# Turning all sixteen heads' probabilities by VectorE and memory in 23 of 48 attention items, with GpSimd making the context's low parts

## The chip, the cores and the metric

The kernel runs on one core of a Trainium2 chip. The metric is the device time of one execution, in microseconds, as the median of several runs. Beside it there is one profiled execution, in which every instruction of the five engines and the transfers are recorded; all rows below are from it.

## What is computed

Sixteen sequences of 128 tokens, width 512, go through a transformer block (self-attention, cross-attention, MLP) and then through a gated cross-attention. All three attentions have 16 heads of 32:

```
def attention(q, k, v, mask):
    scores = jnp.einsum('bhqd,bhkd->bhqk', q, k) / jnp.sqrt(jnp.float32(HD))
    scores = scores * mask - 10000.0 * (1.0 - mask)
    probs = jax.nn.softmax(scores, axis=-1)
    return jnp.einsum('bhqk,bhkd->bhqd', probs, v)
x = x + merge_heads(attention(q, k, v, ltor_mask)) @ w_ao + b_ao      # q, k, v from layernorm(x)
x = x + merge_heads(attention(q, k, v, cross_mask)) @ w_co + b_co     # k, v from the context
x = x + gelu(layernorm(x) @ w1 + b1) @ w2 + b2
out = x + tanh(gate) * (attention with layernorm(context) as k and v) @ Wo
```

## The kernel before

The work is cut into 48 attention items, one sequence in one layer each: items 0 to 15 are the first attention (phase A), 16 to 31 the second (B), then comes the MLP over all sequences, then 32 to 47 the third attention (D). The five engines each run a program written out by hand, and semaphores tie them together. Nothing is scheduled by a planner: the order on each engine is the order of the calls in its `step` function. A product in full precision is made of three: every operand is split into a high part (`context_hi` on ScalarE) and a low part (`context_lo`, which subtracts the high part from the whole), and high times high, high times low and low times high are summed.

A step g works on three items at once. TensorE multiplies the probabilities of item g-2 with v (`times_v`, line 835), makes the scores of item g (`scores`, line 776), projects q, k or v of a later pair of sequences (`project`, lines 750 and 758) with the row sums (line 810) and the transposes (`transpose_prob`, line 794) of item g-1 between, and ends with the output projection of item g-2 (line 858). VectorE masks the scores out of PSUM (line 1590), finds the row maxima (1603), inverts the row sums of item g-1 (`inverse_sums`, 1611), normalises the context of item g-2 (`context`, 1627) and makes its low part (`context_lo`, 1633). In phases A and B GpSimd adds the mask bias (2023) between the mask and the maximum. ScalarE takes 16 exponentials an item (1217), one a head, in four quarters.

Before probabilities can be multiplied with v, the 128x128 block of each head has to be transposed. There are two ways. For heads 0 to 7 ScalarE writes its exponentials into a tile `prob_blocks`, VectorE turns all 32x32 blocks in it with one instruction (`turn_blocks`, 1617), SyncE stores the tile to memory (`store_blocks`, 516) and reads it back with the blocks moved to their places (`bring_blocks`, four DMAs, 525). For heads 8 to 15 TensorE transposes in PSUM (8 instructions) and ScalarE copies the result back with one instruction (`probs_out`, 1194). Items in `BY_PE` use TensorE for all heads. The column order in which the first way leaves the probabilities is read by `times_v` with a stride (`by_head`).

SyncE issues all DMAs from one queue in program order; a wait in it holds everything behind. In step g its order around the change is: the result of item g-3 stored, the turned blocks of item g-1 read back, the row sums of item g-1 stored, the residual of item g-2 loaded, a layer-norm tile loaded in every second step, the row sums of item g-1 spread over the context tile (`spread_row_sums`, 559), then weights or masks, and last the blocks of item g stored and the next inputs read in transposed form.

```
def row_sums(g):
    pe.wait_ge(s_rt, g + 1)
    ...
def inverse_sums(g):
    par = g % 2
    dve.wait_ge(s_exp, 4 * g + 4)
def turn_blocks(g):
    dve.wait_ge(s_exp, 4 * g + 2)
```

## Time and profile before

| | |
|---|---|
| timed runs, median (lowest, highest) | 1100.44 us (1100.13, 1104.86) |
| profiled execution, span from first to last instruction | 1100.7 us |
| TensorE busy in the span | 1074.7 us, 98% |
| VectorE | 815.4 us, 74% |
| ScalarE | 712.7 us, 65% |
| GpSimd | 462.0 us, 42% |
| DMA, mean over the span | 152 GB/s |
| granted TensorE clock | full in every slice |

No time of its own is given for the profiled execution beside its span; the span is 0.3 us above the median of the timed runs. Busy shares are means over the whole span, in which the three attentions and the MLP follow one another; items 2 to 13 lie between 55 and 250 us, items 33 to 43 between 881 and 1055 us. The chain of waits is followed back from the last instruction, at each step to what released it. In the timeline a bracket gives the idle time ahead of a row and who ended it.

### The profile page before, as it was taken

What the parts mean: (1) busy time and instruction counts of PE and PEld (TensorE: products, weight loads), DVE (VectorE), ACT (ScalarE), POOL (GpSimd) and SP (SyncE); (2) the same over time, 40 slices, a digit from 0 to 9 for tenths busy, and PEclk for the clock granted to TensorE, in tenths of its full rate; (3) what the DMA queues carried; (4) which work ended last, traced back from release to release, by engine and by line L of the source; (5) the groups of instructions that cost most, each with busy time, mean ns of one, the idle gap of its engine ahead of it and who ended that gap; (6) DMA issues with size and microseconds to landing.
All of it is one profiled execution on the core that took longest, in us unless ns stands there. A gap on an engine that the chain in (4) does not pass through costs nothing.

```text
span 1100.7 us, 24328 instructions
## 1 busy us (share of the span) xinstructions
PE 1074.7 (98%) x8829; PEld 934.2 (85%) x8829; DVE 815.4 (74%) x1314; ACT 712.7 (65%) x2365; POOL 462.0 (42%) x337
## 2 busy tenths in 40 slices
PE   7989999999999999998999999999999999999998
PEld 6888888888888888886898888888888988888886
DVE  6678787778888778888877557656677478778777
ACT  4678777777788778786444434434444387777776
POOL 3665666557767776767512121103012331122100
PEclk9999999999999999999999999999999999999999
DMA  6366565576776777553241130220622146666633
GB/s 216 98 201 198 191 195 188 174 227 216 221 227 215 223 211 229 180 191 128 85 134 40 38 96 12 85 96 1 181 101 83 59 146 205 203 198 210 177 97 97
DMA packets 136135, 167.04 MB, mean 152 GB/s; under 512 B 16992, under 2 KB 82256, under 8 KB 136016
## 3 DMA queue, kind: packets, MB, share of 16 engines
q1 hardware_dynamic: 136016, 165.50, 47.9%
q8 instruction: 70, 1.15, 0.4%
q14 instruction: 49, 0.40, 0.1%
HBM read 113.15 MB, written 52.29 MB: 150 GB/s over the span
## 4 chain that ended last, share of the span: by engine, by line
PE 59%; DVE 12%; ACT 9%; POOL 7%; issue 4%; DMA 3%; SPq 1%; DVEq 0%; ACTq 0%; POOLq 0%
PE psum L938 15%; PE psum L919 14%; PE psum L758 13%; POOL prob L2023 6%; PE psum L858 5%; PE psum L750 5%; ACT prob L1217 4%; ACT prob_blocks L1217 2%; PE psum L794 2%; PE psum L776 2%; DVE prob L1590 2%; DVE ln_tile L1528 2%; PE psum L835 2%; DVE negmax L1603 2%; ACT inputs_transposed L1255 2%
## 5 line engine op out<-in xcount | busy, mean ns | idle before, releaser
L758 PE MATMUL psum<-inputs_hi,weights_hi 128*128 128x256 f32 x768 | 223.7, 291 | 5.4 <-POOL inputs_lo L2014 2.5
L758 PE MATMUL psum<-inputs_lo,weights_hi 128*128 128x256 f32 x768 | 217.1, 283 | 0.0
L758 PE MATMUL psum<-inputs_hi,weights_lo 128*128 128x256 f32 x768 | 217.0, 283 | 0.0
L2014 POOL TENSOR_TENSOR inputs_lo<-inputs_transposed,inputs_hi 128x512 fp32r<-128x512 f32 x84 | 113.0, 1367 | 228.9 <-DVE inputs_hi L1563 168.4
L2023 POOL TENSOR_TENSOR prob<-prob,mask_bias 128x1024 f32<-128x1024 f32 x64 | 152.7, 2408 | 98.3 <-DVE prob L1590 96.3
L1217 ACT ACTIVATE prob<-prob,negmax 128x128 f32<-128x128 f32 x472 | 182.2, 391 | 0.5 <-DVE negmax L1603 0.5
L758 PEld LDWEIGHTS psum<-inputs_hi,weights_hi 128*128 128x128 f32 x768 | 146.7, 191 | 10.3 <-issue 2.8
L1603 DVE TENSOR_REDUCE negmax<-prob 128x8 f32<-128x1024 f32 x96 | 115.9, 1210 | 50.0 <-POOL prob L2023 50.0
L758 PEld LDWEIGHTS psum<-inputs_lo,weights_hi 128*128 128x128 f32 x768 | 147.0, 191 | 0.2
L758 PEld LDWEIGHTS psum<-inputs_hi,weights_lo 128*128 128x128 f32 x768 | 146.9, 191 | 0.0
L858 PE MATMUL psum<-weights_hi,context_parts 128*128 128x512 f32 x376 | 125.8, 393 | 0.4 <-ACT kT L1168 0.3
L1217 ACT ACTIVATE prob_blocks<-prob,negmax 128x128 f32<-128x128 f32 x296 | 114.4, 389 | 16.9 <-DVE negmax L1603 16.9
L1303 ACT ACTIVATE qT<-psum,columns 128x512 f32<-128x512 f32 (+1 forms) x80 | 46.2, 598 | 106.2 <-PE psum L919 106.2
L1687 DVE SCALAR_TENSOR_TENSOR kT<-kT,qT 128x512 f32<-128x512 f32 x64 | 46.9, 733 | 80.3 <-ACT kT L1308 80.2
L2026 POOL TENSOR_TENSOR residual<-residual,bias_rows 128x512 f32<-128x512 f32 x42 | 57.7, 1378 | 83.3 <-DMA residual<-stream 63.3
L1217 ACT ACTIVATION_READ_ACCUMULATOR prob<-prob,negmax 128x1 f32 x472 | 90.3, 191 | 0.0
L938 PE MATMUL psum<-weights_hi,hidden_parts 128*128 128x512 f32 x264 | 87.7, 392 | 1.1 <-DVE hidden_parts L1682 1.0
L1255 ACT ACTIVATE inputs_transposed<-inputs_transposed,columns 128x256 f32<-128x256 f32 x120 | 62.3, 591 | 37.2 <-DVE inputs_transposed L1535 37.0
L1989 POOL TENSOR_TENSOR weights_lo<-weights_whole,weights_hi 128x512 fp32r<-128x512 f32 x56 | 75.8, 1367 | 21.3 <-ACT weights_hi L1154 21.3
L858 PEld LDWEIGHTS psum<-weights_hi,context_parts 128*128 128x128 f32 x376 | 70.6, 188 | 16.5 <-ACT qT L1303 0.6
L938 PE MATMUL psum<-weights_hi,context_parts 128*128 128x512 f32 x248 | 81.8, 390 | 0.9 <-DVE context_parts L1682 0.9
L1590 DVE SCALAR_TENSOR_TENSOR prob<-psum,mask 128x512 f32<-128x512 f32 x128 | 79.2, 680 | 0.0
(124 smaller groups left out, 2600.3 us busy)
## 6 DMA issues: line engine op xcount, KB each, us to landing
prob_turned<-prob_blocks SPq DMA_DIRECT2D x37, 512.0 KB, 3.0
prob<-prob_turned SPq DMA_DIRECT2D x148, 128.0 KB, 3.3
weights_whole<-weights_in SPq DMA_DIRECT2D x72, 256.0 KB, 3.4
normalised<-ln_tile SPq DMA_DIRECT2D x30, 512.0 KB, 2.8
inputs_transposed<-normalised SPq DMA_DIRECT2D x120, 128.0 KB, 2.9
context<-row_sums_spread SPq DMA_DIRECT2D x188, 64.0 KB, 2.1
stream<-residual SPq DMA_DIRECT2D x42, 256.0 KB, 2.7
residual<-stream SPq DMA_DIRECT2D x42, 256.0 KB, 3.7
```

The costliest lines, as they stand in the source:

```text
L758: mm = pe.matmul(ps[:, bank, GT * part:GT * part + GT], w[:, slot, c, o], a[:, buf, c, :], start=c == 0 and i == 0, stop=c == KC - 1 and i ...
L858: mm = pe.matmul(ps[:, U_BANK + 1, :], a[0][:, cs], w[:, slot, c, :], start=c == 0 and i == 0, stop=c == KC - 1 and i == 2)
L919: mm = pe.matmul(out, w[:, slot, c, o], a, start=c == 0 and i == 0, stop=c == KC - 1 and i == 2)
L938: mm = pe.matmul(ps[:, accumulator(group, t), :], a[gb][:, tok], w[:, slot, (j * chunks + e) % 4, :], start=j == 0 and e == 0 and i == 0, ...
L1217: ins = act.activation(dst, src, ACT.Exp, bias=negmax[:, par, s:s + 1], accum_out=total[:, par, s:s + 1])
L1255: ins = act.activation(dst, src, ACT.Identity, bias=cols[:, b0 + c:b0 + c + 1], scale=cols[:, g0 + c:g0 + c + 1])
L1590: ins = dve.scalar_tensor_tensor(heads(P[:, 512 * c:512 * c + 512]), ps[:, S_BANK:S_BANK + 4, T * c:T * c + T], SCALE, other.unsqueeze(1). ...
L1603: dve.tensor_reduce(negmax[:, par, 8 * h:8 * h + 8], heads(prob[:, par, 1024 * h:1024 * h + 1024]), AX.X, ALU.max, negate=True).then_inc(s ...
L1989: pool.tensor_tensor(wlo[:, slot, c, :], raw[:, slot, c, :], whi[:, slot, c, :].bitcast(f32), ALU.subtract).then_inc(s_wlo, 1)
L2014: pool.tensor_tensor(lo, y, hi.bitcast(f32), ALU.subtract).then_inc(s_rlo if fill.ln is None else s_flo, 1)
L2023: pool.tensor_tensor(half, half, mb.unsqueeze(1).to_broadcast([128, 8, T]), ALU.add).then_inc(s_biased, 1)
L2026: pool.tensor_tensor(tile, tile, brow[:, ROW_SLOT[name], :], ALU.add).then_inc(s_resb, 1)
```

## The change

In the 23 items of `WHOLE` (2 to 13 and 33 to 43) heads 8 to 15 take the first way too. ScalarE writes their exponentials into a second tile, `second_prob_blocks`; VectorE turns it (`turn_second_blocks`) when the item's last quarter of exponentials is done, in the step after; SyncE stores it (512 KB) and reads it back (4 x 128 KB). TensorE's 8 transposes and ScalarE's copy go. The row sums use another PSUM bank and wait for the context of the item before, and `times_v` waits for the second reads. The low part of the context is made by GpSimd, at the start of its step, for items 1 to 13 and 32 to 43 (`LO_BY_POOL`).

```diff
+WHOLE = tuple((*range(2, 14), *range(33, 44)))
+LO_BY_POOL = tuple((*range(1, 14), *range(32, 44)))
...
+        second_blocks = sb("second_prob_blocks", [128, NH // 2 * T])
...
         def row_sum_bank(g):
-            return U_BANK if sums_late(g) else U_BANK + 1
+            return T_BANK + 1 if g in WHOLE else U_BANK if sums_late(g) else U_BANK + 1
...
+            def store_second_blocks(g):
+                n = second_number(g)
+                sp.wait_ge(s_turned2, n)
+                if n > 2:
+                    sp.wait_ge(s_moved2, 64 * (n - 2))
+                sp.dma_start(turned_second[n % 2], second_blocks[:, :]).then_inc(s_pst2, 16)
+
+            def bring_second_blocks(g):
+                n = second_number(g)
+                sp.wait_ge(s_pst2, 16 * n)
+                blocks = turned_second[n % 2].rearrange("(i k) (j n) -> j k i n", i=4, j=4)
+                for j in range(4):
+                    dst = prob[32 * j:32 * j + 32, g % 2, NH // 2 * T:].rearrange("p (i n) -> p i n", i=4)
+                    sp.dma_start(dst, blocks[j]).then_inc(s_moved2, 16)
...
                 if st.prev and g - 1 not in BY_PE:
                     bring_blocks(g - 1)
+                if g - 1 in WHOLE:
+                    store_second_blocks(g - 1)
                 if st.prev:
                     store_row_sums(g - 1)
                 if st.ends:
                     load_stream(g - 2)
                 if st.later and st.later.ln is not None and not ahead_ln and g:
                     load_tiles(st.later)
+                if g - 1 in WHOLE:
+                    bring_second_blocks(g - 1)
                 if st.prev:
                     spread_row_sums(g - 1)
...
                 pe.wait_ge(s_rt, g + 1)
-                if sums_late(g):
+                if g in WHOLE:
+                    pe.wait_ge(s_cx, 2 * g)
+                elif sums_late(g):
...
             def times_v(g):
-                pe.wait_ge(s_pta, copied_by_act(g, 1))
+                if g in WHOLE:
+                    pe.wait_ge(s_rc, g + 1)
+                    pe.wait_ge(s_moved2, 64 * second_number(g))
+                else:
+                    pe.wait_ge(s_pta, copied_by_act(g, 1))
...
-                    else:
+                    elif g - 1 not in WHOLE:
                         transpose_prob(g - 1, 2)
                         if g != 44:
                             transpose_prob(g - 1, 3)
                 if not late:
-                    if st.prev:
+                    if g - 1 in WHOLE:
+                        u_bank_free(g)
+                    elif st.prev:
                         row_sums_out(g - 1)
...
+                second = g in WHOLE and quarter >= 2
+                if second and quarter == 2 and second_number(g) > 1:
+                    act.wait_ge(s_pst2, 16 * (second_number(g) - 1))
...
-                elif st.prev and g != 44:
+                elif st.prev and g != 44 and g - 1 not in WHOLE:
                     probs_out(g - 1)
...
+            def turn_second_blocks(g):
+                dve.wait_ge(s_exp, 4 * g + 4)
+                dve.transpose(second_blocks[:, :], second_blocks[:, :]).then_inc(s_turned2, 1)
...
                 if st.ends and not late:
                     inverse_sums(g - 1)
+                if g - 1 in WHOLE:
+                    turn_second_blocks(g - 1)
+                if st.ends and not late and g - 2 not in LO_BY_POOL:
                     context_lo(g - 2, 0)
                     context_lo(g - 2, 1)
...
             def step(st):
                 phase, b, g = st.phase, st.b, item(st)
+                if g - 2 in LO_BY_POOL:
+                    context_lo(g - 2, 0)
+                    context_lo(g - 2, 1)
                 if phase != D:
                     add_mask_bias(g, 0)
```

How the order moves, at three places. First VectorE in step 9 (context of item 7, row sums of item 8). Before:

```order
L1627 TENSOR_TENSOR context<-psum,context 128x256 x2
L1611 RECIPROCAL rtotal<-total 128x4x4
L1633 TENSOR_TENSOR context_parts<-context,context_parts 128x256 x2
L1590 SCALAR_TENSOR_TENSOR prob<-psum,mask 128x512 x4
L1603 TENSOR_REDUCE negmax<-prob 128x8
L1646 TENSOR_TENSOR v<-psum,bias_rows 128x512
L1603 TENSOR_REDUCE negmax<-prob 128x8
L1528 TENSOR_SCALAR ln_tile<-ln_tile,ln_mean_var,ln_rstd 128x512 x2
L1646 TENSOR_TENSOR v<-psum,bias_rows 128x512
L1617 STREAM_TRANSPOSE prob_blocks<-prob_blocks 128x1024
L1658 TENSOR_TENSOR residual<-psum,residual 128x512
L1627 TENSOR_TENSOR context<-psum,context 128x256 x2
```

and now (line numbers are those of the changed kernel):

```order
L1690 TENSOR_TENSOR context<-psum,context 128x256 x2
L1669 RECIPROCAL rtotal<-total 128x4x4
L1680 STREAM_TRANSPOSE second_prob_blocks<-second_prob_blocks 128x1024
L1648 SCALAR_TENSOR_TENSOR prob<-psum,mask 128x512 x4
L1661 TENSOR_REDUCE negmax<-prob 128x8
L1709 TENSOR_TENSOR v<-psum,bias_rows 128x512
L1661 TENSOR_REDUCE negmax<-prob 128x8
L1586 TENSOR_SCALAR ln_tile<-ln_tile,ln_mean_var,ln_rstd 128x512 x2
L1709 TENSOR_TENSOR v<-psum,bias_rows 128x512
L1675 STREAM_TRANSPOSE prob_blocks<-prob_blocks 128x1024
L1721 TENSOR_TENSOR residual<-psum,residual 128x512
L1690 TENSOR_TENSOR context<-psum,context 128x256 x2
```

The low part of the context stood behind the reciprocal; the turn of the second blocks of item 8 stands there now, ahead of the masks.

Second SyncE's queue in step 37 (items 34 and 36, and the store of item 37's blocks at the end). Before:

```order
L534 DMA result<-residual 128x512
L525 DMA prob<-prob_turned 32x4x256 x4
L551 DMA row_sums_spread<-row_sums_transposed 16x128
L530 DMA residual<-stream 128x512
L454 DMA ln_tile<-enc_in 128x512 x2
L559 DMA context<-row_sums_spread 32x512 x4
L545 DMA mask_rows<-mask_d_in 128x128
L516 DMA prob_turned<-prob_blocks 128x1024
```

and now:

```order
L568 DMA result<-residual 128x512
L544 DMA prob<-prob_turned 32x4x256 x4
L551 DMA second_prob_turned<-second_prob_blocks 128x1024
L585 DMA row_sums_spread<-row_sums_transposed 16x128
L564 DMA residual<-stream 128x512
L473 DMA ln_tile<-enc_in 128x512 x2
L559 DMA prob<-second_prob_turned 32x4x256 x4
L593 DMA context<-row_sums_spread 32x512 x4
L579 DMA mask_rows<-mask_d_in 128x128
L535 DMA prob_turned<-prob_blocks 128x1024
```

The second store stands directly behind the first reads, and the four second reads stand ahead of the spread row sums.

Third TensorE in step 38, around the row sums of item 37. Before:

```order
L758 MATMUL psum<-inputs_hi,weights_lo 128x256
L810 MATMUL psum<-identity,rtotal 16x128
L794 MATMUL psum<-identity,prob 128x128 x8
L758 MATMUL psum<-inputs_hi,weights_hi 128x256
L758 MATMUL psum<-inputs_lo,weights_hi 128x256
```

and now:

```order
L796 MATMUL psum<-inputs_hi,weights_lo 128x256
L850 MATMUL psum<-identity,rtotal 16x128
L796 MATMUL psum<-inputs_hi,weights_hi 128x256
L796 MATMUL psum<-inputs_lo,weights_hi 128x256
```

The eight transposes between the row sums and the next projection are gone.

## Rows read from the trace of the kernel before

**Rows 1.** The page, section 1: busy time, share of the span and instructions of each engine.
```profile
PE 1074.7 (98%) x8829; PEld 934.2 (85%) x8829; DVE 815.4 (74%) x1314; ACT 712.7 (65%) x2365; POOL 462.0 (42%) x337
```
**Rows 2.** Chain of waits in 164 to 198 us: start, length, what.
```profile
166.78 0.48 DVE context_parts L1633 x2
167.46 1.29 DVE prob L1590 x2
168.82 4.77 POOL prob L2023 x2
...
179.99 0.36 DVE context_parts L1633
...
196.17 0.28 PE psum L810
```
**Rows 3.** Busy time by stretch: stretch, length, each engine, clock, DMA share, GB/s.
```profile
55.00:196.00 141.00, 136.89 (x1405) 121.45 (x1399) 108.88 (x172) 108.22 (x421) 87.71 (x58) 1.00 0.60 195
895.00:1055.00 160.00, 158.36 (x1607) 140.16 (x1602) 122.68 (x212) 120.93 (x459) 34.47 (x33) 1.00 0.63 194
```
**Rows 4.** Chain of waits in 953 to 984 us, shares by line.
```profile
by line: PE psum L758 37.7%; PE psum L858 19.1%; PE psum L750 18.5%; PE psum L835 9.8%; PE psum L776 9.2%; PE psum L794 5.6%; PE psum L810 0.7%
```
**Rows 5.** Timeline of TensorE around the transposes of item 37.
```profile
958.41 1.03 PE L794 MATMUL psum<-identity,prob 128*128 128x128 f32 x8
959.20 0.36 PE L758 MATMUL psum<-inputs_hi,weights_hi 128*128 128x256 f32 x1
```
**Rows 6.** Timeline of ScalarE, step 38.
```profile
962.35 0.60 ACT L1168 ACTIVATE kT<-psum 128x512 f32<-128x512 f32 x1 [1.84 <-PE psum L758]
963.88 0.39 ACT L1217 ACTIVATE prob_blocks<-prob,negmax 128x128 f32<-128x128 f32 x1
```
**Rows 7.** VectorE's group of the first blocks' turn: count, busy us, mean ns, idle before.
```profile
L1617 DVE STREAM_TRANSPOSE prob_blocks<-prob_blocks 128x1024 f32<-128x1024 f32 x37 | 45.6, 1233 | 21.2 <-ACT prob_blocks L1217 21.2
```
**Rows 8.** Timeline of VectorE, steps 38 and 39.
```profile
955.16 0.74 DVE L1627 TENSOR_TENSOR context<-psum,context 128x256 f32<-128x256 f32 x2
957.64 0.25 DVE L1611 RECIPROCAL rtotal<-total 128x16 f32<-128x16 f32 x1
967.10 1.25 DVE L1617 STREAM_TRANSPOSE prob_blocks<-prob_blocks 128x1024 f32<-128x1024 f32 x1 [3.12 <-ACT prob_blocks L1217]
```
**Rows 9.** GpSimd: its mask-bias group, and a timeline row of step 38.
```profile
L2023 POOL TENSOR_TENSOR prob<-prob,mask_bias 128x1024 f32<-128x1024 f32 x64 | 152.7, 2408 | 98.3 <-DVE prob L1590 96.3
963.54 2.83 POOL L2014 TENSOR_TENSOR inputs_lo<-inputs_transposed,inputs_hi 128x512 fp32r<-128x512 f32 x2 [9.13 <-ACT inputs_hi L1278]
```
**Rows 10.** Timeline of TensorE: products with v of items 37, 38 and 43; scores of 38.
```profile
954.22 1.17 PE L776 MATMUL psum<-kT,qT 32*128 32x128 f32 x32
967.71 1.08 PE L835 MATMUL psum<-prob,v 128*32 128x128 f32 x32
982.28 1.08 PE L835 MATMUL psum<-prob,v 128*32 128x128 f32 x32
1052.92 1.08 PE L835 MATMUL psum<-prob,v 128*32 128x128 f32 x32
```
**Rows 11.** SyncE's queue: reads of items 37, 38 and 43, and a held issue.
```profile
957.92 1.94 SPq L525 DMA_DIRECT2D prob<-prob_turned  x4
960.26 1.81 SPq L551 DMA_DIRECT2D row_sums_spread<-row_sums_transposed  x1
972.48 2.97 SPq L525 DMA_DIRECT2D prob<-prob_turned  x4
1045.87 1.88 SPq L525 DMA_DIRECT2D prob<-prob_turned  x4
```
**Rows 12.** Issue to landing in us: stores (L516), reads (L525), spreads (KB, median).
```profile
DMA to landing us min/median/max: 2.6/3.0/5.5
DMA to landing us min/median/max: 2.5/3.3/4.9
context<-row_sums_spread SPq DMA_DIRECT2D x188, 64.0 KB, 2.1
```

More of the change, by code:

```diff
@@ L1335, in step @@
                     half_out(*st.units[1])
-                if g == 44:
+                if g == 44 and g - 1 not in WHOLE:
                     probs_out(g - 1)
@@ L1728, in step @@
                 mask_scores(g, 1)
-                if late:
+                if late and g - 2 not in LO_BY_POOL:
                     context_lo(g - 2, 0)
```

33 lines of the change are left out of this document (26 added, 7 removed).

## Prediction

> **What bounds the kernel now.** The profiled execution has a span of 1100.7 us; the three timed runs have a median of 1100.44, so I add my sum to 1100.4. I read the shares first: TensorE is busy 98% of the span, VectorE 74%, GpSimd 42% [rows 1]. That invites the answer that whatever leaves TensorE is won. The share is an average, so I read the chain of waits next, in the two stretches that the change touches. They differ. In the first attention layer, up to 196 us, the chain does not run through TensorE at all: from 166 us it goes VectorE mask, GpSimd mask bias, VectorE maximum and turns, ScalarE exponentials, VectorE again, and TensorE enters only at 196.17 [rows 2]. TensorE idles there about 3% (136.89 busy of 141) [rows 3]; it is fed by that loop, and its high share only says that the two are close. From 196 us on, and all through the third layer, the chain is TensorE alone: in 953 to 984 us it consists of nothing else, and the 8 transposes of each item are links of it [rows 4]. So the first twelve items are split: the work of items 2 to 9 falls under the loop, that of 10 to 13 and of 33 to 43 under TensorE.
>
> **What is removed.** 23 items lose 8 transposes each. The first starts at 958.41 and the next projection at 959.20: 0.79 us an item [rows 5], 23 x 0.79 = 18.2 us off TensorE. That is the most that this change can bring by itself. ScalarE loses one copy an item; in the third layer it waits 1.84 us for TensorE behind that copy [rows 6], in the first layer the chain goes by GpSimd and VectorE while that copy is made [rows 2], so I price this at nothing: the cover is the wait that follows, and nothing is charged if it shrinks.
>
> **What is added on VectorE.** Each item's second turn is the same instruction as the first one, 1.23 us [rows 7]. It stands right behind the reciprocal, where the two context_lo halves stood, 0.68 us from their start to the next mask (166.78 to 167.46) [rows 2]. Net +0.55 us a step. In the first layer this lies on the chain: the chain passes through these very instructions at 166.78 and 179.99 [rows 2]. Steps 3 to 10 (turns of items 2 to 9) thus pay 8 x 0.55 = **+4.4 us**. In the third layer VectorE idles 3.12 us before it turns the blocks of item 38 [rows 8], which hides the 0.55.
>
> **GpSimd.** Two halves of 128x256. Two of its 128x512 subtractions take 2.83 us [rows 9], so the halves take 1.4 if the cost goes by size, 2.8 if it were all fixed. In the first layer it must be over before the mask bias starts. The two halves wait for ScalarE's copies, as VectorE's do now from 166.78; 1.4 us later is 168.2, and the mask bias, at 168.82 now, would start 0.55 later, at 169.4 [rows 2]. With 2.8 us it would be late by 0.2, and by some 0.4 where the copies are later, 12 x 0.4 = 5 us in all. I take 0, because 2.41 us for 128x1024 against 1.4 for half of it shows a cost that goes mostly by size [rows 9], and keep the 5 for the range. In the third layer GpSimd idles 9.13 us at a time [rows 9].
>
> **TensorE's other edits.** Half of the 32 products of an item already read the turned layout; all 32 take 1.08 us [rows 10]. If the second half cost as much as the whole pass again it would be +1 a step; nothing in the record says so, and I take 0. The transpose of the row sums goes to another bank and waits for the context of the item before, which is finished at 955.90, while the transposes behind the row sums start at 958.41 [rows 5, 8]: no cost. The wait for the copied row sums, which stood ahead of the next projection, moves behind a whole step: no gain either, as no idle time stands there.
>
> **The new road through memory.** This decides the third layer. Item 37's exponentials end near 956.8 and VectorE will have turned the second blocks about 959.1 (957.64 + 0.2 + 1.25) [rows 8]. SyncE's queue, in order, then issues one store of 512 KB and four reads back, the reads only when the store has landed. Queue time: the four reads of the first half run from 957.92 to 959.86 [rows 11], and the new store stands behind them, at 959.9. It lands 3.0 us later (2.6 to 5.5), 962.9; the reads then take 1.35 us until the fourth is issued and 3.3 us (2.5 to 4.9) to land [rows 12]: 967.6. TensorE now begins the products of item 37 at 967.71 and without the transposes would want to at 966.9 [rows 10]. So by medians there is nothing left over: 0.1 earlier than now. For item 38 the first reads end at 975.45 [rows 11]; store landed 978.5, reads landed 983.2, against 982.28 now [rows 10]: 0.9 late. Mean +0.4. By the fast ends it is 966.4 and 982.0, by the slow ends 971.7 and 987.3. Behind the reads stand the four spreads of the row sums: for item 37 the last would be issued near 966.1 and land 2.1 us later, 968.2 [rows 12], about when the products that the context needs are done (967.71 + 1.08) [rows 10]: nothing more.
>
> The medians belong to a queue that is now 0.63 busy at 194 GB/s [rows 3]. At full share that is 308 GB/s, 1.7 us for 0.52 MB; the change adds two such loads to each step of 14.5 us, share 0.63 + 3.4/14.5 = 0.86, and already one small issue is held for 1.81 us behind such a burst [rows 11]. Bounds of the extra landing time: 0 and 1.7 for each of the two transfers. I take 0.3 each, nearer the low end since the two wait for each other and seldom overlap. First lateness: 0.4 + 0.6 = **+1.0**.
>
> Then it feeds back. Item g's products come right before the scores of item g+2, whose exponentials make the blocks of g+2; a delay is carried on, and the lateness comes again every second step, less what the road from scores to exponentials can shorten. Now it is 9.66 us (954.22 to 963.88) [rows 6, 10]; VectorE reaches the context 0.94 us after the scores start [rows 8, 10], of which a late TensorE gives back at most 0.8, and the turn takes its 0.55 from it, while the key projection that ScalarE waits for comes 0.79 earlier. I take 0.5 back. So each further pair of steps costs 1.0 - 0.5 = 0.5: items 35 to 42 make about 4.5 pairs, **+2.3**. Item 43 has the least room: its reads end at 1047.75, store landed 1051.1 and reads 1056.1 by the same steps, against 1052.92 now [rows 10, 11]: +3.2, of which 1.0 is counted, **+2.2**. Third layer: +5.5.
>
> In the first layer items 10 to 13 save TensorE's 4 x 0.79 = **-3.2**. Item 13 is the last there and I charge it the same first lateness as an item of the third layer, **+1**. The earlier items are late too, but TensorE has slack under the loop there.
>
> Sum: 4.4 - 3.2 + 1 + 1.0 + 2.3 + 2.2 = +7.7, 1100.4 + 7.7 = **1108**. About 0.5% is what a measurement can tell from no change here, so this lies just outside it.
>
> **The Trainium skill** would make the road shorter. "DMA: Bandwidth & Descriptors" (the section with the fit of time to bytes) gives a transfer about 2.0 us plus its bytes over 436 GB/s. An estimate by that page: store 3.2 us, one read of 128 KB 2.3 us, so the blocks of item 37 would be there at 959.9 + 3.2 + 1.35 + 2.3 = 966.8, just as TensorE wants them. The store agrees with our median, the read does not (3.3 in the trace), and the measurement decides; but the page speaks for the first rival below.
>
> **The rivals.**
> *TensorE gets its time.* The transfers land at their fast ends and the third layer gains 0.79 for each of 11 items, 8.7 us, the first layer 3.2 less part of the loop's 4.4. For it: the last read of item 37's first half is issued at 959.4, lands about 962.7 by the median and is needed 5 us later, and the fast ends of the new road reach 966.4 [rows 10 to 12]. The loop's cost may also be less, if a VectorE wait for GpSimd shrinks. 1100.4 - 8.7 - 3.2 = 1088.5 with a free loop, 1093 with the whole. I say 1090. Against it: both medians are slower. It decides if store and reads together take under 7.0 us from the store's issue (959.9 to 966.9). Chance 0.20.
> *Only the loop counts.* Transfers at the median without the queue's extra: third layer 0 to +2, first layer +1.2. 1101 to 1104. Chance 0.20.
> *The queue saturates.* Landings grow by 1.7 us each: lateness 0.4 + 3.4 = 3.8, each pair of steps 3.3, capped since bursts spread as steps grow longer; half of that, 1.9 + 4.5 x 1.4 + 2.2 + 1.5 = 11.9 in the third layer, 5 in the first with GpSimd late as well: 17 to 22, 1120. For it: the held issue, and landings of 5.5 in the record [rows 11, 12]. Chance 0.18.
> *The forecast*, 1103 to 1116, has the remaining 0.42.
> That the edit does not do what it says is excluded by the order of the instructions: the 8 transposes are gone from all 23 items.
>
> **How the numbers follow.** Faster by over 0.5% (under 1094.9) takes the first rival: 0.20. Within 0.5% (to 1105.9) takes the second and the low end of the forecast, 0.20 + 0.08 = 0.28. Slower: 0.34 + 0.18 = 0.52. The range leaves out half of the first rival and half of the last: 1090 to 1121.
>
> **What would show it.** In the changed profile: the transposes' group down from 456 to 272; in 953 to 984 us a TensorE that waits for the DMA of the second blocks before its products, some 1 to 2 us a step, and a step of 14.6 to 15 us against 14.5; VectorE's chain in the first layer longer by 1.1 us per pair of steps, so that TensorE takes over the chain about 4 us later than 196; a DMA share of about 0.85 in the third layer. I am wrong if TensorE still fills the third layer's chain, without a DMA in it and with steps under 14 us: then the road had room that I did not see. I am wrong the other way if steps exceed 15.5 us.

## The result and the profile after

The change takes 1152.76 us (1149.18 to 1153.69, 4 runs) against 1100.33 us for the kernel before on the same chip: ratio 1.0458, 95% interval 1.0430 to 1.0486. That is 52 us slower, where 8 were forecast, and beyond the range that ended at 1121. The profiled execution took 1153.6 us.

Page of the change: section 1, TensorE's clock in 40 slices, queue 1 (packets, MB, share of 16 engines), the chain that ended last, and three kinds of DMA issues (KB each, median us to landing).
```profile
span 1152.3 us, 24095 instructions
PE 1076.1 (93%) x8645; PEld 933.3 (81%) x8645; DVE 822.9 (71%) x1287; ACT 693.7 (60%) x2342; POOL 499.4 (43%) x387
...
PEclk9998999998999999999999999999999998889999
...
q1 hardware_dynamic: 152576, 189.62, 53.5%
...
PE 53%; DMA 10%; DVE 10%; ACT 8%; issue 6%; SPq 6%; POOL 4%; DVEq 0%; ACTq 0%; POOLq 0%
...
prob_turned<-prob_blocks SPq DMA_DIRECT2D x37, 512.0 KB, 3.7
...
second_prob_turned<-second_prob_blocks SPq DMA_DIRECT2D x23, 512.0 KB, 4.2
prob<-second_prob_turned SPq DMA_DIRECT2D x92, 128.0 KB, 3.0
```
Busy time by stretch, of the change, the same columns as in [rows 3].
```profile
55.00:196.00 141.00, 126.24 (x1223) 111.68 (x1212) 106.42 (x156) 92.06 (x374) 94.27 (x70) 0.94 0.74 234
895.00:1055.00 160.00, 142.66 (x1328) 126.20 (x1327) 113.66 (x181) 102.95 (x402) 49.02 (x51) 0.94 0.68 208
937.00:1105.00 168.00, 145.31 (x1367) 127.62 (x1370) 118.12 (x185) 102.58 (x413) 45.03 (x48) 0.92 0.77 234
```
TensorE, 158.36 us busy of 160 in the third layer before [rows 3], is busy 142.66 now, and in the first layer 126.24 of 141 against 136.89. The DMA share rose from 0.60 to 0.74 in the first layer. Items 33 to 43 lie later in the changed kernel, in 937 to 1105 us; the last row is for them alone, with TensorE idle for 22.7 us and a DMA share of 0.77. From the products of item 2 to those of item 13 the profiled execution is 21.3 us longer, and from item 33 to 43 24.3 us: 45.6 of the 51.6 that its span grew. So most of the time sits in the two stretches that were edited, as idle TensorE.

Groups of the change: the transposes, the second turn, the products (busy us, mean ns, idle before them).
```profile
L832 PE MATMUL psum<-identity,prob 128*128 128x128 f32 x272 | 35.4, 273 | 0.0
...
L1680 DVE STREAM_TRANSPOSE second_prob_blocks<-second_prob_blocks 128x1024 f32<-128x1024 f32 x23 | 27.3, 1188 | 1.6 <-ACT second_prob_blocks L1275 1.6
...
L887 PE MATMUL psum<-prob,v 128*32 128x128 f32 x1504 | 58.3, 302 | 46.0 <-issue 40.3 <-DMA prob<-second_prob_turned 5.7
```
184 transposes are gone and the turn costs what it was said to. The last row holds the result: TensorE idles 46.0 us in front of the products (23.8 in the first layer, 22.0 in the third). "issue" is idle time that the profile gives to nobody; the next rows show what it is: waits for the second reads to land.

Timelines of the change around item 36: SyncE's queue, then TensorE (start, length, what, idle before).
```profile
972.45 0.33 SPq L535 DMA_DIRECT2D prob_turned<-prob_blocks  x1
976.15 1.81 SPq L505 DMA_DIRECT2D inputs_transposed<-normalised  x4
978.01 0.45 SPq L568 DMA_DIRECT2D result<-residual  x1
978.50 1.89 SPq L544 DMA_DIRECT2D prob<-prob_turned  x4
980.48 0.38 SPq L551 DMA_DIRECT2D second_prob_turned<-second_prob_blocks  x1
...
985.86 1.75 SPq L559 DMA_DIRECT2D prob<-second_prob_turned  x4
987.71 1.76 SPq L593 DMA_DIRECT2D context<-row_sums_spread  x4
```
```profile
955.66 1.94 PE L887 MATMUL psum<-prob,v 128*32 128x128 f32 x32 [4.78 <-issue]
957.53 2.09 PE L814 MATMUL psum<-kT,qT 32*128 32x128 f32 x32
971.78 1.08 PE L887 MATMUL psum<-prob,v 128*32 128x128 f32 x32
972.79 1.17 PE L814 MATMUL psum<-kT,qT 32*128 32x128 f32 x32
990.58 1.93 PE L887 MATMUL psum<-prob,v 128*32 128x128 f32 x32 [5.02 <-issue]
```
VectorE has turned item 36's second blocks at 976.8. The store stands in SyncE's queue behind the reads of the next inputs (held until 976.15, when the normalised tiles had landed in memory), a result store and the four reads of the first blocks, and goes out at 980.48. The store of the first blocks had landed at 977.3, before its reads came up, so here it is the queue and not that landing that holds. The second store lands at 985.8, the reads go out at once, the last lands at 990.5, and the products start at 990.58. The products of items 34, 38, 40 and 42 also start within 0.1 us of that landing, and in the first layer those of the odd items 3 to 13. Between them lie items whose products start 0.2 to 1.7 us after their landing, with TensorE busy until then: one wait falls on every second item. From S(36), the start of item 36's scores, to S(38) the loop is 17.2 us (957.5 to the last exponential, 974.7), 15.9 (the road to the products) and 1.8 (to 992.4): 34.9 us for two steps. Before, from item 38 to 40, it is 16.4 + 11.7 + 1.0 = 29.1. The pairs from S(38) and S(40) take 32.9 and 33.5 in the change.

For odd items the road is nearly as long (from the last exponential to the landing 13.7 to 15.5 us in items 35 to 41), for another reason. Timeline of VectorE in the change, item 37, whose exponentials ended at 990.1.
```profile
992.57 0.42 DVE L1690 TENSOR_TENSOR context<-psum,context 128x256 f32<-128x256 f32 x1 [0.43 <-PE psum L887]
...
994.60 1.29 DVE L1648 SCALAR_TENSOR_TENSOR prob<-psum,mask_bias 128x512 f32<-128x512 f32 x2 [0.86 <-PE psum L814]
995.80 0.25 DVE L1669 RECIPROCAL rtotal<-total 128x16 f32<-128x16 f32 x1
995.96 1.19 DVE L1680 STREAM_TRANSPOSE second_prob_blocks<-second_prob_blocks 128x1024 f32<-128x1024 f32 x1
```
The turn of item 37 stands behind the context of item 36, which waits for the late products, and behind the first mask of item 38, which waits for the scores after them. It is done 7.1 us after the exponentials instead of 2.3.

The edit has one more wait: ScalarE may not overwrite the second blocks before the store of the item before has landed. It holds nothing up. In every item the store has landed 1.1 us (item 37) or more before ScalarE comes to those exponentials, and ScalarE does not idle in front of them.

**The granted clock.** Granted clock (before the DMA share) in a stretch of the change.
```profile
988.00:993.00 5.00, 2.42 (x40) 2.07 (x44) 3.40 (x8) 2.54 (x13) 1.26 (x3) 0.55 0.73 232
```
After idling 5.02 us TensorE runs at half of 2.4 GHz: the 32 products take 1.93 us and the scores after them 2.09, where they take 1.08 and 1.17 at full clock. There are eleven such stretches in the two layers, 58 us in all, each at a wait of 3.0 us or more for the landing or right behind one; the kernel before has none. "TensorE: Matmul & The Clock Gate" of the Trainium skill (Part 1, the two states) names 1.2 and 2.4 GHz for an idle and a busy engine; the trace agrees. Whether this costs time is for an experiment to say.

### The profile page after: what moved, and what is told of

The parts are those of the page before. It is cut to its first block, busy times and chain, and to the rows that moved or that the text cites. A ratio compares the mean times of both kernels' runs of the same rounds, so it can differ in the third digit from the quotient of the medians.

```text
span 1152.3 us, 24095 instructions
## 1 busy us (share of the span) xinstructions
PE 1076.1 (93%) x8645; PEld 933.3 (81%) x8645; DVE 822.9 (71%) x1287; ACT 693.7 (60%) x2342; POOL 499.4 (43%) x387
## 4 chain that ended last, share of the span: by engine, by line
PE 53%; DMA 10%; DVE 10%; ACT 8%; issue 6%; SPq 6%; POOL 4%; DVEq 0%; ACTq 0%; POOLq 0%
PE psum L990 14%; PE psum L971 14%; PE psum L796 11%; PE psum L910 4%; PE psum L788 4%; POOL prob L2094 4%; ACT prob L1275 3%; DMA normalised<-ln_tile 3%; PE psum L814 2%; DMA second_prob_turned<-second_prob_blocks 2%; PE psum L887 2%; ACT prob_blocks L1275 2%; DVE ln_tile L1586 2%; DMA prob_turned<-prob_blocks 2%; SPq L544 2%
## 5 line engine op out<-in xcount | busy, mean ns | idle before, releaser
L796 PE MATMUL psum<-inputs_hi,weights_hi 128*128 128x256 f32 x768 | 226.5, 295 | 4.8 <-POOL inputs_lo L2080 2.9
L2080 POOL TENSOR_TENSOR inputs_lo<-inputs_transposed,inputs_hi 128x512 fp32r<-128x512 f32 x84 | 112.4, 1361 | 182.5 <-DVE inputs_hi L1621 136.1
L796 PEld LDWEIGHTS psum<-inputs_hi,weights_hi 128*128 128x128 f32 x768 | 149.1, 194 | 11.2 <-issue 5.0
L1275 ACT ACTIVATE prob<-prob,negmax 128x128 f32<-128x128 f32 x288 | 111.2, 391 | 0.0
L887 PE MATMUL psum<-prob,v 128*32 128x128 f32 x1504 | 58.3, 302 | 46.0 <-issue 40.3
L887 PEld LDWEIGHTS psum<-prob,v 128*32 128x32 f32 x1504 | 44.5, 120 | 63.0 <-issue 62.9
```

The source lines that it names most:

```text
L796: mm = pe.matmul(ps[:, bank, GT * part:GT * part + GT], w[:, slot, c, o], a[:, buf, c, :], start=c == 0 and i == 0, stop=c == KC - 1 and i ...
L887: mm = pe.matmul(out, vv[:, gp, half, h * HD:h * HD + HD], P, start=True, stop=True)
L1275: ins = act.activation(dst, src, ACT.Exp, bias=negmax[:, par, s:s + 1], accum_out=total[:, par, s:s + 1])
L2080: pool.tensor_tensor(lo, y, hi.bitcast(f32), ALU.subtract).then_inc(s_rlo if fill.ln is None else s_flo, 1)
```

## The experiments

Ratios are to the kernel before on the same chip, with 95% intervals. Diffs are against the change unless another kernel is named. Two spans serve all of them: from the start of item 2's products to those of item 13, and from item 33's to item 43's, each in the profiled execution. The medians are from several chips, so compare the ratios. A profiled execution is one of the timed ones and not always near their median: that of first_only was the slowest of four (1131.8 us), those of no_turn (1089.5) and stores_first (1135.6) the fastest.

| kernel | median us | ratio | 2 to 13 | 33 to 43 |
|---|---|---|---|---|
| before | 1100.3 | 1 | 162.0 | 143.4 |
| the change | 1152.8 | 1.0458 [1.0430, 1.0486] | 183.3 | 167.7 |
| no_road | 1102.2 | 1.0008 [0.9988, 1.0028] | 160.7 | 139.7 |
| no_turn | 1093.2 | 0.9930 [0.9906, 0.9954] | 154.8 | 140.1 |
| pool_only | 1102.5 | 0.9989 [0.9968, 1.0011] | 159.6 | 144.1 |
| lo_by_dve | 1154.1 | 1.0462 [1.0427, 1.0497] | 182.5 | 166.5 |
| filler | 1152.1 | 1.0440 [1.0418, 1.0461] | 180.4 | 166.2 |
| turn_first | 1154.3 | 1.0458 [1.0437, 1.0480] | 182.1 | 167.1 |
| first_only | 1126.1 | 1.0221 [1.0177, 1.0265] | 186.8 | 143.9 |
| third_only | 1122.4 | 1.0180 [1.0141, 1.0218] | 159.6 | 165.1 |
| road_unwaited | 1120.4 | 1.0171 [1.0113, 1.0229] | 159.6 | 164.1 |
| load_only | 1113.1 | 1.0088 [1.0062, 1.0113] | 159.6 | 154.1 |
| quarter_free | 1103.1 | 1.0005 [0.9990, 1.0020] | 159.6 | 143.9 |
| quarter_size | 1119.9 | 1.0148 [1.0112, 1.0184] | 163.9 | 153.5 |
| first_quarter | 1127.3 | 1.0220 [1.0196, 1.0245] | 173.6 | 153.3 |
| stale_reads | 1143.2 | 1.0379 [1.0347, 1.0411] | 177.9 | 163.4 |
| stores_first | 1141.8 | 1.0399 [1.0354, 1.0445] | 175.8 | 158.4 |
| act_store | 1141.2 | 1.0379 [1.0341, 1.0416] | 177.4 | 159.4 |
| act_queue | 1145.7 | 1.0406 [1.0372, 1.0439] | 178.4 | 162.9 |
| even_only | 1111.7 | 1.0078 [1.0054, 1.0101] | 159.6 | 154.0 |

**Which part costs: no_road, pool_only, lo_by_dve.** The first leaves out the second store and its reads (the products of heads 8 to 15 of the 23 items then read what the masks left), the second keeps only GpSimd's new work, the third only takes that work back.
```
no_road:    -    store_second_blocks(g - 1)
            -    bring_second_blocks(g - 1)
            -    pe.wait_ge(s_moved2, 64 * second_number(g))
            +    pe.wait_ge(s_turned2, second_number(g))
            -    act.wait_ge(s_pst2, 16 * (second_number(g) - 1))
            +    act.wait_ge(s_turned2, second_number(g) - 1)
pool_only:  +WHOLE = ()
lo_by_dve:  +LO_BY_POOL = ()
```


> The changed kernel without the second store and the four second reads in all 23 items: the products with v wait for VectorE's turn alone and read the second half of prob as the masks left it, so the results for heads 8 to 15 are not those of the reference. Everything else stays: VectorE's second turn, GpSimd's low parts, TensorE without the transposes. Theory ROAD (TensorE waits each step for the second blocks to come back from memory, and its clock falls in the wake of those waits): no wait, no low clock, so 1100 - 18 + 4 = about 1086 us, granted clock 1.00. Rival ENGINES (VectorE's added turn and GpSimd's context_lo are what the time went to): stays near 1150. Rival CLOCK ALONE (the clock falls for another reason than waits): mean granted clock stays near 0.975 and the time above 1110.

> The kernel before with nothing but GpSimd's context_lo for items 1 to 13 and 32 to 43 (no item takes the second road). VectorE's chain in the first layer loses 0.68 us a step, some ten steps: 1093 to 1097 us if GpSimd's two halves hide ahead of the mask bias; 1100 if TensorE takes over at once; over 1105 if GpSimd's halves are late for the mask bias or slow VectorE.

> The changed kernel with the context's low part back on VectorE everywhere. If the road decides, the move to GpSimd is worth VectorE's 0.68 us a step at most, and VectorE's context and turn are on the loop: 1152 to 1168. If GpSimd's low parts are part of the loss (late for the output projection or the mask bias), the time falls below 1148.


Without the road the 52 us are gone, and with them the low clock (0.998). GpSimd's part changes nothing that the times can tell in either kernel; in the profiled executions pool_only's first layer is 2.4 us shorter (159.6), and the kernels that edit the third layer alone have the same 159.6. But no_road doesn't gain TensorE's 18 us either.

**What eats the 18 us: no_turn.** no_road, without the two waits for VectorE's second turn, and
```
-    turn_second_blocks(g - 1)
```


> As no_road (no second store, no second reads), and VectorE's second turn is left out too; the products of heads 8 to 15 read probabilities that are neither moved nor turned. TensorE has the 8 transposes of 23 items less (18.2 us). If VectorE's added turn of 1.23 us a step is what kept no_road at 1102 us: 1083 to 1090 us. Rival: the 18 us did not come because the loop of mask, exponentials and projections was as long as TensorE's work all along, and the turn is hidden: 1098 to 1103 us.


It is 8.6 us faster than no_road by the ratios (0.9930 against 1.0008), 5.9 of it between items 2 and 13, while the third layer doesn't move (139.7 and 140.1). So VectorE's second turn lies on the loop of the first layer and is hidden in the third, as was forecast. Of the 18.2 us that leave TensorE some 8 (by the ratio; 12 in the profiled execution, its fastest) become time even when VectorE and the queue get no new work. The chain of waits in no_turn's trace shows what ends last then. In 893 to 1050 us its largest parts are landings that SyncE's queue waits for (normalised tiles 12.5%, row sums 9.6%, the next tiles' load 8.8%) and that queue's own issues; TensorE's projections have 7.6%, where the kernel before has nothing but TensorE there [rows 4]. In 55 to 245 us the largest part is GpSimd's mask bias, 22.5%. So in the third layer a loop through SyncE's queue stood close behind TensorE even before a byte was added.

**Is it the clock: filler.** 24 transposes of the identity, results unused, ahead of the wait for the second reads.
```
+    for k in range(24):
+        pe.transpose(ps[:, T_BANK + 1, ...], ident[:, :], ident[:, :])
     pe.wait_ge(s_moved2, 64 * second_number(g))
```


> The changed kernel with 24 transposes of the identity (some 2.4 us of TensorE work whose result nobody reads) before the wait for the second blocks, in each of the 23 items. If the half clock that follows the waits costs what the trace suggests (TensorE works 48 us of the 59.5 us at half clock, 24 us lost), keeping TensorE at work in the wait keeps the clock up and gives back 10 to 24 us: 1130 to 1142 us, mean clock over 0.99. If the clock does not matter, the waits absorb the filler and the time stays at 1152 or rises by a few us; if the waits were not waits for memory, it rises by 23 x 2.4 = 55.


Span and clock of filler:
```profile
core 0: 1150.2 us, clock 0.996
```
The clock is back (0.996, the change 0.975), the time is not: 1.0440 against 1.0458, with intervals that overlap. With no_road's clock of 0.998 this says that the slow clock comes from the waits and is not what the 52 us are. It does not say that it costs nothing, since the filler is not free.

Timeline of TensorE in filler, item 36.
```profile
981.19 2.78 PE L868 MATMUL psum<-identity 128*128 128x128 f32 x24
984.06 1.08 PE L889 MATMUL psum<-prob,v 128*32 128x128 f32 x32
985.07 1.17 PE L814 MATMUL psum<-kT,qT 32*128 32x128 f32 x32
```
In the third layer it mostly fits into the wait: item 36's products start right at the landing and the scores after them 1.0 us later instead of 1.9, but the landing itself comes later after the exponentials (15.9 us on the mean of items 34, 36, 38, 40 and 42, the change 15.0), so the wait takes back most of what the clock gives. In the first layer its 2.78 us also stand in front of items for which TensorE did not wait: item 12's products start 3.5 us after the landing instead of 0.5. What the clock alone costs there is not separated.

**Is it VectorE's order: turn_first.** VectorE makes the reciprocal and the second turn at the head of the step, ahead of the context; they go from their old places.
```
+    if g - 1 in WHOLE:
+        inverse_sums(g - 1)
+        turn_second_blocks(g - 1)
     if st.ends and not late:
         context(g - 2, 0)
```


> The changed kernel with VectorE's inverse of the row sums and the second turn of item g-1 moved to the head of its step, ahead of the context of item g-2 and the first mask. Theory ONE-STEP LOOP (products of item g-1 -> VectorE's context or mask -> turn of item g -> store -> reads -> products of item g): the turn no longer waits for the products of the item before, in the third layer it comes up to 5 us earlier in odd items (960.9 against exponentials done at 955.3), so steps of 16.8 us fall to 15 to 15.5: 1115 to 1130 us. If the loop is not what sets the step (the first reads ahead in the queue hold the store anyway), the time stays within 1145 to 1155.


No change (1.0458 both). Timeline of turn_first, item 37: VectorE's turn and SyncE's queue.
```profile
988.08 1.19 DVE L1680 STREAM_TRANSPOSE second_prob_blocks<-second_prob_blocks 128x1024 f32<-128x1024 f32 x1
...
987.41 0.39 SPq L535 DMA_DIRECT2D prob_turned<-prob_blocks  x1
991.74 1.81 SPq L544 DMA_DIRECT2D prob<-prob_turned  x4
993.65 0.38 SPq L551 DMA_DIRECT2D second_prob_turned<-second_prob_blocks  x1
```
The blocks are turned at 989.3 and stored at 993.65: what VectorE no longer holds, the queue does. Two waits of about the same length lay side by side, and one of them alone is worth nothing.

**The layers apart: third_only, first_only.**
```
third_only: +WHOLE = tuple(range(33, 44))
first_only: +WHOLE = tuple(range(2, 14))
```


> The changed kernel with the second road for items 33 to 43 alone. The trace of the changed kernel gives the third layer 24.6 us of the 51.6 (products of item 33 to 43 take 167.7 us against 143.4) and the first layer 24: so 1122 to 1128 us if the layers add up.

> The changed kernel with the second road for items 2 to 13 alone: 1120 to 1128 us if the two layers add up to the whole 52.


They cost 20 and 24 us by the ratios, and in the two spans 21.7 and 24.8, together near what the whole change adds there (24.3 and 21.3). By the ratios the sum is 44 of the whole's 50 us, which the three intervals allow. So the layers add up within the noise, and the third can be studied alone.

**Landing, queue or bytes: road_unwaited, load_only, quarter_free.** All three are third_only with heads 8 to 15 not moved: the reads go to a tile that nobody uses then, and the products wait for VectorE's turn.
```
road_unwaited: +dst = whi[32 * j:32 * j + 32, 7, 0:2, :] ...
               +pe.wait_ge(s_turned2, second_number(g))
load_only, besides:
               +k = max(n - 1, 1)
               +sp.wait_ge(s_pst2, 16 * k)
               +blocks = turned_second[k % 2] ...
quarter_free, besides:
               +sp.dma_start(turned_second[n % 2][0:32, :], second_blocks[0:32, :])
               +sp.dma_start(dst[:, 0:1, :], blocks[j][:, 0:1, :])
```


> As third_only, but the four second reads go to a place that nobody reads and the products wait for VectorE's turn instead of the reads; results for heads 8 to 15 of items 33 to 43 are not the reference's. All transfers and their place in SyncE's queue stay. Theory ROAD LATENCY (what costs is that the products wait for the landing): falls from third_only's 1125 to about 1092 to 1098. Rival QUEUE LOAD (the added 1 MB a step delays the other transfers and SyncE's order, and those delays cost by themselves): stays at 1110 or more.

> Third layer's 11 items alone, to be read beside third_only (1122 us) and road_unwaited (1120 us). As road_unwaited (the reads go to a tile that nobody uses, the products wait for VectorE's turn alone, heads 8 to 15 are thus not moved), and besides the reads fetch the item before's blocks, so that SyncE's queue waits for no second landing either: every byte moves and nothing waits for it. If the road costs by its waits: 1100 to 1106 us. If it costs by its bytes: 1114 to 1120 us.

> load_only (third layer alone, nothing waits for the second road's landings) with a quarter of the bytes; heads 8 to 15 of items 33 to 43 are not moved. If bytes and waits are the whole cost and add up: the products of items 33 to 43 span 141 to 145 us (no_road 139.7, load_only 154.1) and the time is 1098 to 1103 us. If issuing five more transfers a step in SyncE's queue costs by itself: 148 or more, 1107 us or more.


TensorE waits for no landing of second blocks in road_unwaited, and nearly all stays lost (164.1 against third_only's 165.1). Its idle time has moved: not to the products, but to the row sums, 21.3 us in 895 to 1080 us, where it waits for VectorE's reciprocal and so for exponentials that come late. SyncE's queue waits for no second landing either in load_only, and half of the loss is back: 154.1. With a quarter of the bytes besides, quarter_free is at 143.9, the kernel before (143.4). So five more issues a step cost nothing as long as they are small; the bytes cost 10.2 us when nothing waits for them, and the waits the other 11.0 (165.1 less 154.1).

What bytes cost when nobody waits for them shows in load_only's stretch and chain of waits.
```profile
895.00:1055.00 160.00, 143.41 (x1374) 125.43 (x1375) 122.81 (x194) 103.04 (x414) 46.00 (x50) 0.97 0.83 245
```
```profile
961.93 4.28 DMA row_sums_spread<-row_sums_transposed
966.58 0.42 SPq L594
...
968.50 3.96 DMA normalised<-ln_tile
972.90 0.44 SPq L505
...
974.87 0.43 SPq L544
...
981.11 4.75 DMA ln_tile<-enc_in
```
The chain hardly touches TensorE: it goes round SyncE's queue, from the row sums' small store over the normalised tiles' store to the next tiles' load, each in turn waited for. In 920 to 1060 us these three landings make 43% of it, and a large part of the rest are SyncE's own issues. At a share of 0.83 the 64 KB spreads land in 3.1 us (2.0 in the kernel before, both in 900 to 1060 us) and the residual loads in 5.3 (3.4). In the kernel before, the chain in this layer is TensorE alone [rows 4]; so a loop that was hidden under TensorE's step came out.

**The waits with few bytes: quarter_size, first_quarter.** The whole change, with quarter_free's small sizes and all the waits of the change; first_quarter has them on top of stores_first (below). Three quarters of heads 8 to 15 are not moved.
```
+    sp.dma_start(turned_second[n % 2][0:32, :], second_blocks[0:32, :])
+    sp.dma_start(dst[:, 0:1, :], blocks[j][:, 0:1, :])
```


> The change with the same waits and instructions in the same order, but the second store writes 32 of 128 partitions (128 KB) and each read fetches a quarter (32 KB); three quarters of heads 8 to 15 are thus not moved. If the road costs by its bytes: near no_road, 1102 to 1110 us. If it costs by its waits in series: store and reads still take some 2 us each to land (the spreads of the row sums, of 64 KB, take 2.1), the road is about 13 us against 15.9, the loop over two steps 32 us: 1120 to 1130 us.

> stores_first (second store ahead of the first blocks' reads, VectorE turns early) with the quarter sizes of quarter_size. Both causes are cut: by the theory of waits the road is some 10 us, the loop 28.9 us, as long as before's 28.7: 1100 to 1108 us. If it stays above 1115, a third thing costs: the issue time of five more transfers a step in SyncE's queue, or VectorE's order.


Issues of quarter_size: KB each, median us to landing.
```profile
second_prob_turned<-second_prob_blocks SPq DMA_DIRECT2D x23, 128.0 KB, 3.3
prob<-second_prob_turned SPq DMA_DIRECT2D x92, 32.0 KB, 1.8
```
The third layer takes 153.5: 9.6 us over quarter_free, near the 11.0 of the waits above. Taking the bytes away gives 10.2 us without the waits and 11.6 with them, so the two shares nearly add up. The first layer is nearly free (163.9 against no_road's 160.7), so there the size makes 19 of 23 us, in transfers that are waited for: no run of the first layer has the bytes without the waits. first_quarter missed: with VectorE's new order and SyncE's stores first, the first layer is 9.7 us worse than in quarter_size and the third the same. Its first reads wait for the second turn, and context and mask stand behind the turn; that this makes the order pay only where the road is long is argued, not shown.

**One wait at a time: stale_reads, stores_first, act_store, act_queue.** stale_reads has load_only's edit of the reads in the whole change (the products of heads 8 to 15 get the item before's blocks). The others have turn_first's order, and: stores_first issues the second store ahead of the first reads; act_store issues it from ScalarE's queue; act_queue puts the reads there too.
```
stores_first: +    if g - 1 in WHOLE:
              +        store_second_blocks(g - 1)
                   if st.prev and g - 1 not in BY_PE:
                       bring_blocks(g - 1)
act_store:    +act.wait_ge(s_turned2, n)
              +act.dma_start(turned_second[n % 2], second_blocks[:, :])
act_queue:    +act.wait_ge(s_pst2, 16 * n)
              +act.dma_start(dst, blocks[j]).then_inc(s_moved2, 16)
```


> This kernel stores and reads back as many bytes as the change, with the same instructions in the same order, but the four reads fetch the second blocks of the item before (already landed), so SyncE's queue never waits for the second store to land; the products of heads 8 to 15 thus use the wrong item's probabilities. Theory of the queue's waits in series (first store lands, four reads, second store lands, four reads, all in one in-order queue, 15.9 us from the last exponential of item 36 to its products): the wait of 3.3 to 5.3 us goes, the road is about 11.5 us, the loop over two steps about 30.6 us against 34.9, so about two thirds of the 52 us come back: 1117 us (1108 to 1125). Rival, the load of the DMA engines (24 MB more, busy share 0.75 against 0.63): the bytes are the same, so 1145 us or more.

> As turn_first (VectorE turns the second blocks before the context), and SyncE issues the second store ahead of the first blocks' four reads, so both stores are in flight at once. Theory of waits in series: the second store goes out 2.3 us after the last exponential instead of 5.8, both have landed at about +6.5, eight reads take 3.6 us to issue and 2.9 to land: products at about +12.5 to +13 instead of +15.9, the loop over two steps 31.5 to 32 us against 34.9 and 28.7 before: 1125 us (1112 to 1135). Rival, load: two stores at once only collide, each lands later, no change: 1150 us or more.

> As turn_first, and the second store is issued by ScalarE on its own DMA queue as soon as VectorE has turned the blocks; SyncE's queue still issues all reads in the same order. Theory of waits in series: the second store no longer stands behind the landing of the first one and its reads; it lands at about +6.5 after the last exponential, reads issued to +8.3, landed at +11.2 instead of +15.9: 1117 us (1106 to 1128). Rival, load: 1150 us or more. A third way, ScalarE now waits at the head of each step for VectorE's turn: the exponentials would start later and the gain would be given back, 1135 to 1150.

> The whole change with the second store and its four reads issued by ScalarE on its own DMA queue (store at the head of the step, reads ahead of the exponentials), VectorE turning early as in turn_first. If SyncE's single queue is what makes the waits cost: nothing of its order changes against the kernel before, store landed at about +6.5 after the last exponential, reads issued at about +8.8 and landed at +12: products 33 to 43 in 152 to 158 us, 1125 to 1138 us in all. If ScalarE pays 1.8 us a step for issuing, as SyncE does: 1140 to 1155 us.


Each gives back 6 to 9 us by the ratios, where 15 to 35 were expected. stores_first does shorten the loop of item 36 as worked out: 31.7 us from S(36), 946.2, to S(38), 977.9 (the pair after it takes 33.2), and 158.4 in the third layer. What was expected wrongly is the rest: its reads still take 5.0 us from the last issue to landing in item 36, and the first layer, at 175.8, stays far above the 160.7 of no_road. A second queue is no cure. "DMA: Bandwidth & Descriptors" of the Trainium skill (Issuing engines are not separate DMA queues) says that transfers of all issuing engines end up on the same 16 engines; the runs agree: in act_queue's 900 to 1060 us SyncE's first reads land in 4.5 us (3.4 before) and ScalarE's store in 4.7. The time of act_queue also lies in the range that was expected if ScalarE pays for issuing (1140 to 1155), and that of act_store in the one for a ScalarE that waits for the turn (1135 to 1150); these runs do not tell the two reasons apart.

**A part of it for free: even_only.** stores_first, with five items.
```
+WHOLE = (34, 36, 38, 40, 42)
```


> stores_first, but only items 34, 36, 38, 40 and 42 are turned whole by VectorE. TensorE is spared 5 x 0.79 = 4 us. If a road that fits into its step is free: 1097 to 1100 us. If each road costs by its late landing (12.5 us after the last exponential against 10.8 in the kernel before, 1.7 once per two steps, less the 0.8 spared): 1101 to 1106 us. As much per item as stores_first (42 us over 23 items): 1109 us.


9 us for five items, 1.7 an item where stores_first pays 1.9: in this order no item's road is free, not even every second one's. No version that computes the whole reference beats the kernel before; pool_only comes level with it.

## Why the prediction was wrong

Its direction held, and so did the picture of what carries the two layers and the form of the loss: a loop over two steps through store, reads, products and scores. The sizes in that loop failed.

1. *TensorE, 0.79 us an item.* Right as work (456 to 272 transposes), and rightly called the most there is; no_turn got some 8 of 18.
2. *VectorE +4.4 in the first layer, hidden in the third.* Held, near enough: the turn alone costs 5.9 between items 2 and 13 (no_turn against no_road) and the low parts give 2.4 back (pool_only), 3.5 net; in the third layer nothing.
3. *GpSimd 0.* Held (pool_only, lo_by_dve).
4. *Queue time of the second store.* For odd items the text put it at once behind the first reads, 0.8 us after the turn. In the changed kernel that holds only because VectorE is later still: the turn comes 7.1 us after the exponentials, not 2.3, since the context and the mask ahead of it wait for late products and scores. I took the reciprocal's time from the trace of before. turn_first shows that the queue would have held item 37's store 4.4 us in its place. For even items the text's times give 2.6; measured are 3.7 in item 36 and 2.4 to 3.1 in 34, 38, 40 and 42.
5. *Landing 3.0 and 3.3, plus 0.3 each.* Measured medians 4.2 and 3.0, together 7.2 where 6.9 was taken; item 36's store took 5.4. So the added transfers' own landings are not what failed in the main. What their bytes do to the transfers of all others was given no term.
6. *Each further pair of steps costs 0.5.* **This is the step that failed.** The pair of item 36 costs 34.9 - 29.1 = 5.8: the road is longer by 15.9 - 11.7 = 4.2, and of the time from scores to exponentials nothing is given back, it takes 0.8 more; from products to scores the half clock adds 0.8. On the mean of the pairs from items 36, 38 and 40 it is 4.7, of which 3.1 are the road. The text had 1.0 for the road and 0.5 given back. I had let a late TensorE shorten the rest of the loop. Instead the late products hold up the context and the turn behind it, as VectorE's timeline shows, and the store waits its turn in SyncE's queue.
7. *"Behind the reads stand the four spreads: nothing more."* The other failed step. An in-order queue with a new wait of a landing in it delays all that it issues later: road_unwaited and load_only put 10 to 11 us of the third layer's 21 on waits, though TensorE waited for none of them in road_unwaited.
8. *The first layer is covered by the loop, +1.* It lost 23 us (no_road to the change). That it had slack was read from TensorE's 3% idle. The trace shows the same wait as in the third layer: TensorE idles 3.0 to 5.7 us in front of the products of each odd item from 3 to 13, 23 us in all, and starts them when the second reads have landed. 19 of the 23 hang on the transfers' size; whether by their own landings or by those of others was not separated there.

The rival *the queue saturates* named the right cause of half of the third layer's loss and capped it at 22 us, by the argument that bursts spread as steps grow. They did not: the share is 0.74 in the first layer with steps of 16.7 us, and 0.77 in the third. As said ahead, steps over 15.5 us prove the forecast wrong the other way: they are 16.8. The direction was right by the road's terms, 1 + 1.0 + 2.3 + 2.2 = 6.5 us of the 7.7; from no_road to the change the road costs 50.

## What to carry to other kernels

Before a round trip through memory is added to a pipelined kernel, write out the whole loop that it closes, with every wait and issue of its in-order queue, and compare its length with the steps that it spans; what is added beyond the slack is paid in every step and not once. Price its bytes by what all the other transfers of the step then wait for, as well as by its own landing: here half of the third layer's loss came from transfers that nobody waited for. And test such a loss by two cuts at once (sizes and waits), since with equal waits side by side taking one away can show nothing.

## What the hardware showed

- At a DMA share of 0.83 and 245 GB/s (load_only) the landings of 64 KB transfers took half as long again as before (2.0 to 3.1 us), and the third layer was 10 us longer than with a quarter of the added bytes (share 0.70), with the same waits.
- TensorE's clock fell to half in eleven stretches behind waits (one of 5.02 us shown above); restoring it with filler work gave back nothing that can be told (1.0440 against 1.0458), but the filler's 2.78 us an item are part of that.
- Issuing the four second reads took 1.7 to 2.0 us of SyncE's queue in the change, yet five more small issues a step were free (quarter_free, 1.0005).
